# Looking up row numbers for four token tiles per product: diagonal blocks picked by a mask, moved by one small product

## What is computed

```python
capacity = max(1, int(CF * N / E))            # 1.25 * 4096 / 8 = 640
order = jnp.lexsort((-fw, fe))                # by expert, then by falling weight
se, sw, st = fe[order], fw[order], ft[order]  # expert, weight, token
rank = jnp.arange(N * K) - starts[se]
keep = rank < capacity
disp = jnp.zeros((E, capacity + 1, D)).at[se, pos].set(xf[st])
g = jnp.einsum('ecd,edf->ecf', disp, wg)
u = jnp.einsum('ecd,edf->ecf', disp, wu)
eo = jnp.einsum('ecf,efd->ecd', jax.nn.silu(g) * u, wd)
out = jnp.zeros_like(xf).at[st].add(gathered * weight)
```

## Time and profile before

| | |
|---|---|
| median of 3 runs | 659.88 us (659.63 to 659.9) |
| the profiled execution | 656.8 us |
| its span, first to last instruction | 654.9 us |
| TensorE busy | 569.0 us, 87% |
| VectorE busy | 448.4 us, 68% |
| ScalarE busy | 322.0 us, 49% |
| GpSimd busy | 266.4 us, 41% |

### The profile page before, as it was taken

How to read it: one execution, slowest core, us unless ns; L and a number is a source line. 1 busy time by engine, 2 the same in 40 slices (tenths; PEclk the granted TensorE clock), 3 DMA queues, 4 the chain that set the end, 5 groups by cost and what they waited for, 6 DMA issues and landing times.

```text
span 654.9 us, 13692 instructions
## 1 busy us (share of the span) xinstructions
PE 569.0 (87%) x4041; PEld 529.9 (81%) x4041; DVE 448.4 (68%) x1250; ACT 322.0 (49%) x717; POOL 266.4 (41%) x428
## 2 busy tenths in 40 slices
PE   4999889999899401399999999999999999999992
PEld 3677678888777300299999999999999999999992
DVE  3577879898677888875756676677567666666441
ACT  3678768887445510044434445445355354454330
POOL 5588747786678400402025043061070250341321
PEclk9999989999899655589999999999999999999997
DMA  5322258744565640232617336347056174260221
GB/s 169 97 66 73 72 155 269 220 145 132 170 188 189 209 105 0 71 108 82 193 51 159 109 89 137 92 104 185 24 118 195 33 155 129 82 137 9 34 25 16
DMA packets 91911, 75.24 MB, mean 115 GB/s; under 512 B 12108, under 2 KB 88278, under 8 KB 91864
## 3 DMA queue, kind: packets, MB, share of 16 engines
q1 hardware_dynamic: 82872, 58.77, 29.7%
q0 software_dynamic: 8992, 15.90, 12.6%
HBM read 52.48 MB, written 22.16 MB: 114 GB/s over the span
## 4 chain that ended last, share of the span: by engine, by line
PE 63%; DVE 12%; issue 4%; POOL 2%; DMA 2%; ACT 2%; SPq 1%; DVEq 0%; ACTq 0%; POOLq 0%
PE bank L1354 29%; PE bank L1368 14%; PE bank L1389 4%; DVE hit L895 3%; PE bank L1272 3%; PE bank L1175 3%; PE bank L1317 3%; PE bank L1403 2%; PE bank L1331 1%; DVE x L864 1%; PE bank L1252 1%; DVE st L866 1%; DMA w_raw<-wd 1%; PE bank L1261 1%; DMA xg<-h_rows,g_idx 1%
## 5 line engine op out<-in xcount | busy, mean ns | idle before, releaser
L500 POOL DMA_INDIRECT xg<-h_rows,g_idx x40 | 40.8, 1019 | 256.5 <-DVE g_idx L989 246.7
L1354 PE MATMUL bank<-xT_h,w_h 128*128 128x320 f32 x448 | 139.4, 311 | 1.2 <-DVE xT_l L1018 1.2
L1354 PE MATMUL bank<-xT_h,w_l 128*128 128x320 f32 x448 | 138.4, 309 | 0.0
L1354 PE MATMUL bank<-xT_l,w_h 128*128 128x320 f32 x448 | 138.4, 309 | 0.0
L656 ACT CAST hid_h<-hid 128x320 fp32r<-128x320 f32 x112 | 51.7, 461 | 82.5 <-DVE hid L1046 82.5
L1046 DVE TENSOR_TENSOR hid<-act_g,bank 128x320 f32<-128x320 f32 x112 | 54.5, 487 | 54.4 <-ACT act_g L652 54.4
L510 POOL DMA_INDIRECT out<-yo,s_idx x40 | 66.3, 1657 | 60.7 <-DVE yo L1036 21.9
L652 ACT ACTIVATE act_g<-bank 128x320 f32<-128x320 f32 x112 | 48.9, 437 | 82.0 <-PE bank L1354 81.4
L1354 PEld LDWEIGHTS bank<-xT_h,w_h 128*128 128x128 f32 x448 | 84.8, 189 | 1.8 <-issue 1.4
L1354 PEld LDWEIGHTS bank<-xT_l,w_h 128*128 128x128 f32 x448 | 84.6, 189 | 0.0
L1354 PEld LDWEIGHTS bank<-xT_h,w_l 128*128 128x128 f32 x448 | 84.5, 189 | 0.0
(11 more groups left out here) (190 smaller groups left out, 1296.0 us busy)
## 6 DMA issues: line engine op xcount, KB each, us to landing
w_raw<-wg SPq DMA_DIRECT2D x32, 256.0 KB, 3.5
w_raw<-wu SPq DMA_DIRECT2D x32, 256.0 KB, 4.6
w_raw<-wd SPq DMA_DIRECT2D x16, 512.0 KB, 5.7
x_in<-x SPq DMA_DIRECT2D x32, 128.0 KB, 2.1
q_store<-qT SPq DMA_DIRECT2D x32, 128.0 KB, 1.9
q_in<-q_store SPq DMA_DIRECT2D x32, 128.0 KB, 2.1
x_re<-x SPq DMA_DIRECT2D x32, 128.0 KB, 2.1
out<-x SPq DMA_DIRECT2D x32, 128.0 KB, 1.9
```

The costliest lines, as they stand in the source:

```text
L500: nc.gpsimd.indirect_dma_start(out=xg[par][:, a, :], out_offset=None, in_=h2_rows, in_offset=bass.IndirectOffsetOnAxis(ap=g_idx[par][:, a: ...
L1354: last = MM(bank[2 * h + m][:, 0:HCAP], W[i][:, f, at:at + P], XT[j][:, k, cols], start=n == 0, stop=n == 3 * KC - 1)
```

## The change

A slot is now divided by 32 instead of 128: 20 blocks (`BLOCKS`) of 32 rows (`ROWS`). `onehot` has 32 columns per token instead of 128, so the one-hot rows of four token tiles (`Q`) lie side by side as the 128 weight columns of one product, and `facts`, now 2 x 20 = 40 numbers per token tile (`BAND`), of the same four tiles are the 160 streamed columns. A look is 8 products. In the 128 x 160 result only the four diagonal blocks mean something: rows 32q to 32q + 31 with the 40 columns of the q-th tile. `find_diagonal` on VectorE multiplies with the mask `own_q` (`band`) and adds the four blocks (`diag`, 128 x 40). `place` on TensorE, one product with `same_r` (a one wherever two rows are equal modulo 32), sums over the four row groups and gives every group the result. `find_tokens` picks for each row group its column out of four (`spot`, again with `own_q`) and adds the two values.

`own_q`, `fold` and `same_r` are made once on VectorE during attention. ScalarE's copy `iota_b`, a table of 128 x 32 numbers that the old `onehot` was compared with, falls away. `facts_d` counts two parts per expert instead of four.

```diff
-TILE_BITS = 7
+ROWS = 32
+ROW_BITS = 5
+BLOCKS = CAP // ROWS
+Q = P // ROWS
+BAND = NV * BLOCKS
...
+                if s.rep == NT + 5:
+                    with nc.allow_low_precision(reason="zeros and ones"):
+                        RED(own_q[:, :], ident.rearrange("p (q r) -> p q r", q=Q), AX, ALU.add)
+                        link(RED(fold[:, :], ident.rearrange("p (q r) -> p r q", q=Q), AX, ALU.add))
+                    V.tensor_copy(same_r[:, :].rearrange("p (q r) -> p q r", q=Q),
+                                  fold[:, :].unsqueeze(1).to_broadcast([P, Q, ROWS]))
...
-                TT(in_tile[:, :, :], tile_no[:, :].unsqueeze(2).to_broadcast([P, NT, CT]),
-                   tile_id[:, :].unsqueeze(1).to_broadcast([P, NT, CT]), ALU.is_equal).then_inc(in_d, 1)
+                TT(in_block[:, :, :], block_no[:, :].unsqueeze(2).to_broadcast([P, NT, BLOCKS]),
+                   block_id[:, :].unsqueeze(1).to_broadcast([P, NT, BLOCKS]), ALU.is_equal).then_inc(in_d, 1)
...
-                TT(facts[:, sl, :, :], vals[:, sl, :].unsqueeze(3).to_broadcast([P, NT // 2, NV, CT]),
-                   in_tile[:, sl, :].unsqueeze(2).to_broadcast([P, NT // 2, NV, CT]), ALU.mult)
+                TT(facts[:, sl, :, :], vals[:, sl, :].unsqueeze(3).to_broadcast([P, NT // 2, NV, BLOCKS]),
+                   in_block[:, sl, :].unsqueeze(2).to_broadcast([P, NT // 2, NV, BLOCKS]), ALU.mult)
...
-                sl = slice(part * NT // 4, (part + 1) * NT // 4)
-                TT(onehot[:, :, sl], iota_b[:, :, sl], row_in[:, sl].unsqueeze(1).to_broadcast([P, P, NT // 4]),
-                   ALU.is_equal).then_inc(facts_d, 1)
+                sl = slice(part * NT // 2, (part + 1) * NT // 2)
+                TT(onehot[:, sl, :], iota_s[:, 0:ROWS].unsqueeze(1).to_broadcast([P, NT // 2, ROWS]),
+                   row_in[:, sl].unsqueeze(2).to_broadcast([P, NT // 2, ROWS]), ALU.is_equal).then_inc(facts_d, 1)
...
+            def find_diagonal(e):
+
+                dve.wait_ge(look_d, e + 1)
+                TT(band[:, :, :], bank[7][:, 0:Q * BAND].rearrange("p (q n) -> p q n", q=Q),
+                   own_q[:, :].unsqueeze(2).to_broadcast([P, Q, BAND]), ALU.mult).then_inc(band_d, 1)
+                dve.wait_ge(band_d, e + 1)
+                with nc.allow_low_precision(reason="seven bits of each row number are whole and exact"):
+                    RED(diag[:, :], band[:, :, :].rearrange("p q n -> p n q"), AX, ALU.add).then_inc(diag_d, 1)
+
             def find_tokens(e, par):
 
-                dve.wait_ge(look_d, e + 1)
+                dve.wait_ge(place_d, e + 1)
+                TT(spot[:, :].rearrange("p (m q) -> p m q", q=Q),
+                   bank[7][:, Q * BAND:(Q + 1) * BAND].rearrange("p (m q) -> p m q", q=Q),
+                   own_q[:, :].unsqueeze(1).to_broadcast([P, BAND // Q, Q]), ALU.mult).then_inc(spot_d, 1)
+                dve.wait_ge(spot_d, e + 1)
                 with nc.allow_low_precision(reason="row numbers under 4096 are whole and exact"):
-                    RED(g_idx[par][:, :], bank[7][:, 0:NV * CT].rearrange("p (v a) -> p a v", v=NV), AX, ALU.add)\
+                    RED(g_idx[par][:, :], spot[:, :].rearrange("p (v a q) -> p a v q", v=NV, q=Q), AXY, ALU.add)\
                         .then_inc(idx_d, 1)
...
+                    if f == 1 and first:
+                        find_diagonal(1)
+                    if f == FC - 1 and ahead:
+                        find_diagonal(e + 2)
...
-                for n in range(NT):
-                    if n % (NT // 4) == 0:
-                        wait(pe, facts_d, e * 4 + n // (NT // 4) + 1)
-                    last = MM(bank[7][:, 0:NV * CT], onehot[:, :, n], facts[:, n, :, :].rearrange("p v a -> p (v a)"),
-                              start=n == 0, stop=n == NT - 1)
+                for n in range(0, NT, Q):
+                    if n % (NT // 2) == 0:
+                        wait(pe, facts_d, e * 2 + n // (NT // 2) + 1)
+                    last = MM(bank[7][:, 0:Q * BAND], onehot[:, n:n + Q, :].rearrange("p n r -> p (n r)"),
+                              facts[:, n:n + Q, :, :].rearrange("p n v a -> p (n v a)"), start=n == 0, stop=n == NT - Q)
                 last.then_inc(look_d, 1)
+
+            def place(e):
+
+                wait(pe, diag_d, e + 1)
+                MM(bank[7][:, Q * BAND:(Q + 1) * BAND], same_r[:, :], diag[:, :], start=True, stop=True).then_inc(place_d, 1)
...
             look(0)
+            place(0)
...
                     if f == 2 and first:
-                        wait(pe, idx_d, 1)
-                        look(1)
+                        place(1)
...
                 down(e, FC - 1)
+                if ahead:
+                    place(e + 2)
                 gate_up(e + 1, 1 - par, 1)
...
             gate_up(0, 0, 1)
+            pe.wait_ge(idx_d, 1)
+            look(1)
             down(0, 0)
```

More of the change, by code:

```diff
@@ L22 @@
 AX = mybir.AxisListType.X
+AXY = mybir.AxisListType.XY
 B, T, D = 2, 2048, 256
@@ L149, in build_program @@
         same_e = sb("same_e", [P, P], BF16)
+        own_q, same_r = sb("own_q", [P, Q], BF16), sb("same_r", [P, P], BF16)
+        fold = sb("fold", [P, ROWS])
+        band, spot = sb("band", [P, Q, BAND]), sb("spot", [P, BAND])
+        diag = sb("diag", [P, BAND], BF16)
         before, zeros_b = sb("before", [P, P], BF16), sb("zeros_b", [P, P], BF16)
@@ L184, in build_program @@
         vals = sb("vals", [P, NT, NV], BF16)
-        iota_b = sb("iota_b", [P, P, NT], BF16)
-        tile_id = sb("tile_id", [P, CT], I32)
-        in_tile = sb("in_tile", [P, NT, CT])
-        tile_no = sb("tile_no", [P, NT], I32)
+        block_id = sb("block_id", [P, BLOCKS], I32)
+        in_block = sb("in_block", [P, NT, BLOCKS], BF16)
+        block_no = sb("block_no", [P, NT], I32)
         row_in = sb("row_in", [P, NT], BF16)
-        onehot = sb("onehot", [P, P, NT], BF16)
-        facts = sb("facts", [P, NT, NV, CT], BF16)
+        onehot = sb("onehot", [P, NT, ROWS], BF16)
+        facts = sb("facts", [P, NT, NV, BLOCKS], BF16)
         g_idx = [sb(f"g_idx{i}", [P, CT], I32) for i in range(2)]
@@ L297, in build_program @@
         in_d, tn_d, ri_d = sem("in_d"), sem("tn_d"), sem("ri_d")
+        band_d, diag_d, place_d, spot_d = (sem(n) for n in ("band_d", "diag_d", "place_d", "spot_d"))
         facts_d, look_d, idx_d = (sem(n) for n in ("facts_d", "look_d", "idx_d"))
@@ L620, in _ @@
             exp_logits(EARLY, NT)
-            act.wait_ge(plink_s, 8)
-            nc.scalar.copy(iota_b[:, :, :], iota_s[:, :].unsqueeze(2).to_broadcast([P, P, NT])).then_inc(iota_d, 1)
             def split_high(e, f, count, implied=False):
@@ L950, in _, with describe_blocks @@
             place_slots(0)
-            def describe_tiles(e):
+            def describe_blocks(e):
                 sl = slot[:, e, :]
-                V.tensor_scalar(tile_no[:, :], sl, TILE_BITS, None, ALU.arith_shift_right).then_inc(tn_d, 1)
+                V.tensor_scalar(block_no[:, :], sl, ROW_BITS, None, ALU.arith_shift_right).then_inc(tn_d, 1)
                 dve.wait_ge(tn_d, e + 1)
-                TT(in_tile[:, :, :], tile_no[:, :].unsqueeze(2).to_broadcast([P, NT, CT]),
-                   tile_id[:, :].unsqueeze(1).to_broadcast([P, NT, CT]), ALU.is_equal).then_inc(in_d, 1)
-                V.scalar_tensor_tensor(row_in[:, :], tile_no[:, :], -float(P), sl, ALU.mult, ALU.add).then_inc(ri_d, 1)
+                TT(in_block[:, :, :], block_no[:, :].unsqueeze(2).to_broadcast([P, NT, BLOCKS]),
+                   block_id[:, :].unsqueeze(1).to_broadcast([P, NT, BLOCKS]), ALU.is_equal).then_inc(in_d, 1)
+                V.scalar_tensor_tensor(row_in[:, :], block_no[:, :], -float(ROWS), sl, ALU.mult, ALU.add).then_inc(ri_d, 1)
             def describe_facts(e, part):
@@ L1004, in split_low @@
                 V.tensor_tensor(w_l[:, f, :], w_raw[:, f, :], w_h[:, f, :].bitcast(F32), ALU.subtract).then_inc(sp_l, 1)
[L1006 removed]
             describe(0)
+            find_diagonal(0)
             find_tokens(0, 0)
@@ L1056, in describe_ahead @@
                     if f == 2:
-                        describe_tiles(e + 2)
+                        describe_blocks(e + 2)
                     if f in (3, 4):
@@ L1061, in describe_ahead @@
                         describe_rows(e + 2, 0)
+                        describe_rows(e + 2, 1)
                 xf = FC - XG if first else XF
@@ L1066, in expert @@
                     if f == 0 and first:
-                        describe_tiles(1)
+                        describe_blocks(1)
                         describe_facts(1, 0)
-                    if f == 1 and first:
-                        describe_rows(1, 1)
-                        describe_rows(1, 2)
                     if f == 0 and not first:
@@ L1084, in expert @@
                         describe_rows(1, 0)
-                    if f == 1 and first:
-                        describe_rows(1, 3)
```

(7 more changed lines are left out.)

7 lines of the change are left out of this document (2 added, 5 removed).

## The result

The changed kernel takes 651.13 us (median of 9 runs, 649.07 to 655.14), the kernel before beside it 659.67 us (9 runs, 655.35 to 662.85): a ratio of 0.988, 95% interval 0.9861 to 0.9899. The profiled execution took 651.43 us, with a span of 649.3 us.

What follows compares the result with a forecast made beforehand. TensorE, busy 87% of the span and alone on the chain in the middle experts, was taken as the bound. Terms 0.7 + 1.6 + 0.35 - 1.4 - 6.0 = -4.75 us gave 655.1 us from 659.88 us, range 652.0 to 658.2 us.

Steps and rivals of the forecast that it cites:

- the last of the sum: Whole kernel: 652.05 us from the profiled execution, plus the 3.1 us between profile and median, gives 655.1 us.
- Middle experts: Five looks between full experts: each falls from 2.05 to 0.86 us, saving 1.2 us; together -6.0 us.
- Third look: Look behind the wait for expert 1's weights: shorter look, wait unchanged, -1.4 us.
- Routing: First look, serial: nothing covers VectorE's longer work and the four waits in a row, +1.6 us.
- Expert 0: Second look's saving lost to VectorE's queue, with stalls of 0.4 us for `hid`, 0.7 us for `diag`: +0.35 us.
- another rise of the clock there: Start of expert 0: sign of being wrong if the clock, at half until about 282 us, rose at another point.
- Masks: Building `own_q`, `fold`, `same_r` on VectorE in attention, in a chain without slack: +0.7 us (0.3 to 0.8 us).
- The prices: VectorE instructions at the slow rate: `in_block` and `facts` 0.82 us each, `onehot` 0.69 us, `diag` 0.32 us.
- (1): VectorE: fast rate holds for `facts` and `onehot`, helping first look and expert 0; -7.2 us, 652.7 us; 12%.
- (2): TensorE: wide product costs as much as one of 256 columns, `place` 0.4 us; -1.15 us, 658.7 us; 9%.
- (3): TensorE: the new products' weight loads are not hidden, a look takes 3.0 us; +9.9 us, 669.8 us; 4%.
- The lower bound of the product: Look on TensorE: eight products of 160 columns cost at least 8 x 0.062 = 0.5 us.

Runs made afterwards that it cites:

- before: The kernel before, unchanged, in the profile the prediction was made from: profiled execution 656.8 us, span 654.9 us.
- b_again: The kernel before, unchanged, timed and profiled once more: 659.19 us, ratio 1.0009; profile span 656.7 us.
- b_third: The kernel before, unchanged, profiled a third time: one execution, 660.8 us, span 658.9 us.
- after: The changed kernel in its first profile: profiled execution 651.43 us, span 649.3 us; median of runs 651.13 us, ratio 0.988.
- a_again: The changed kernel, unaltered, timed and profiled once more: 650.17 us, ratio 0.987 to the kernel before.
- a_pad: The changed kernel with its new buffers placed behind the old ones, so the others keep their earlier addresses: 649.83 us, ratio 0.9875 to the kernel before.
- a_twice: The changed kernel with every look done twice, 16 products for 8: 656.1 us, ratio 0.9955 to the kernel before.
- b_fourth: The kernel before, unchanged, profiled once more, on the third chip: clock 0.66 behind the third look, `gate_up` there 4.86 us.
- b_wide: The kernel before with 160 streamed columns in each of a look's 32 products, 150 of them unread: 660.71 us, ratio 1.0033.
- b_fifth: The kernel before, unchanged, a further profile: clock 0.70 behind the third look, `gate_up` there 5.16 us.
- b_warm: The kernel before with 12 unread products of 256 columns filling part of the wait ahead of the third look: 658.14 us, ratio 0.999.
- a_spread: The changed kernel with expert 1's list, look and `place` in expert 0 in the old order: 648.78 us, ratio 0.9852 to the kernel before.
- a_early: The changed kernel with the masks built at the program's start instead of late in attention: 650.38 us, ratio 0.9873 to the kernel before.
- a_fast: The changed kernel with the four token tiles innermost in every 2-byte buffer: 648.23 us, ratio 0.9848 to the kernel before.
- a_fill: The changed kernel with 24 unread products of 10 columns ahead of the third look: 652.72 us, ratio 0.9898 to the kernel before.
- a_comb: The changed kernel with token tiles innermost, `in_block` from 2-byte numbers and expert 0's old order, third chip: 654.6 us, ratio 0.9798 to the kernel before.

## Why the prediction was wrong

The stages, in us from the span's start, and what lies between:

| | before | b_again | b_third | after | a_again |
|---|---|---|---|---|---|
| thresholds known (`thr_b`) | 261.3 | 260.5 | 262.9 | 262.2 | 261.6 |
| first `hid` | 283.8 | 282.9 | 285.3 | 286.2 | 285.8 |
| third look | 326.16 | 326.27 | 328.55 | 328.73 | 328.76 |
| last `hid` of the full experts | 597.0 | 598.9 | 601.1 | 591.4 | 591.5 |
| routing | 22.5 | 22.4 | 22.4 | 24.0 | 24.2 |
| expert 0 | 42.4 | 43.4 | 43.3 | 42.5 | 43.0 |
| middle experts | 270.8 | 272.6 | 272.6 | 262.7 | 262.7 |

**The step that failed** is the last of the sum: "the median of the runs is 659.88 us, 3.1 us more, and I take the difference over". The profiled execution of before was not the typical one plus a constant. It lay near the lower end: leaving out the third chip, the kernel before runs from 655.35 to 663.42 us, and its further profiles took 658.68 and 660.8 us. What it lacked did not come back after the change: after, profile and median are 651.43 and 651.13 us. Against its own base the sum gave 652.05 us, within 1 us of both; in part that is luck, since the terms below miss by up to 0.5 us each and in both directions. In place of 3.1 us to carry over, the runs showed that a good part of the difference is a gain:

- The half clock behind the third look costs 4.92 - 3.62 = 1.3 us to 1.5 us, in five of six profiles of kernels with narrow looks there, and the changed kernel doesn't have it. The prediction asks after the clock at the first look and at the start of expert 0 only.
- The period of a middle expert, (552.8 - 371.75) / 4 = 45.26 us by the starts of the looks in my profile, is 45.42 us in the two others: 0.16 us x 5 = 0.8 us. The looks add up to the same; 32 and 33 of the `down` there take 1.77 us, where 21 did in my profile and the rest 1.73 us. The changed kernel shows such a step too (43.97 us, but 43.89 us in `a_pad`). Why it differs stays open.
- Expert 0 takes 42.4 us in my profile and 43.3 us in the others, in part between the request for expert 1's weights and their use (14.8, 15.2 and 15.6 us in the three, 14.4 us after). Over all profiles that wait takes 14.8 to 16.1 us with the narrow look and 14.0 to 15.7 us in the six with the changed order. It scatters from run to run, and that the change has a part in it is not shown. In `b_again` another 0.5 us comes from a clock that rose late (see the terms).

So 1.3 to 1.5 us of the 3.1 us are a gain with a cause, 0.8 us have a place in the traces and no cause, and the rest is not told from scatter.

**The terms.** Middle experts: -6.0 us forecast. The period fell from 45.26 us to (548.65 - 372.77) / 4 = 43.97 us, 1.29 us instead of 1.2 us, so -6.5 us; against 45.42 us it is -7.3 us. The product was right (0.069 us by `a_twice`, the line through the two rows gave 0.068 us, I took 0.075 us); `place` costs 0.13 us for 0.15 us. Mis-sized was what the look takes off the `gate_up` behind it: that is 3.56 us now and not 3.62 us, since the products before it are wide.

Third look: -1.4 us forecast, 2.15 + 3.62 - 0.73 - 3.56 - 0.13 = 1.35 us measured. Routing: +1.6 us forecast, +1.5 to +1.8 us measured. Expert 0: +0.35 us forecast; the stalls were 0.37 us for `hid` and 0.48 us for `diag` (0.4 and 0.7 us forecast), and from the first `hid` to the transposes at f = 5 it is 28.1 us, against 27.6, 28.1 and 27.7 us. The middle one is `b_again`, where the granted clock reached 1.00 only behind the first `hid` (0.50 over the 5 us ahead of it, 0.80 in the first microsecond behind); so it was in `b_fourth` (28.4 us) and `b_wide` (28.5 us), while in `before`, `b_third`, `b_fifth` and `b_warm` (27.6 to 27.7 us), and in all ten kernels with the new look, it stood at 1.00 by then. Like with like the stretch is 0.5 us longer after the change, near the forecast 0.35 us, and `a_spread` (27.1 us) shows that the order is what eats the gain. The prediction had named another rise of the clock there as a sign of being wrong; it moves some executions of before, not the changed kernel.

Masks: +0.7 us forecast (0.3 to 0.8 us), 0.4 us in the traces. By the starts of `st`, thirteen tiles at the end of attention take 35.3 to 35.4 us in all nine profiles that build the masks there, and 34.9 to 35.0 us in `a_early` and in all but one of the profiles with the old look (35.1 us in `b_fifth`). The three instructions keep VectorE for 0.8 us; half of that falls into time in which its `x` would have waited for TensorE (0.26 to 0.39 us at the tiles beside), which the forecast took as not there. `a_early` was not faster for it: its last tile waited for a transfer, so that it stands 3.25 us behind the tile before, where it is 2.4 to 3.4 us in the profiles of the other kernels with the new look, without a pattern.

**The prices.** `in_block`, `facts` and `onehot` came at 825, 818 and 684 ns, as forecast at the slow rate; `a_fast` confirms the reason by removing it. With that the rule of the Trainium skill ("Vector Engine (DVE) Microarchitecture Reference", section 5.1), an innermost step of one for the packed mode, agrees with the runs on both sides. `diag` was 439 ns and not 320 ns: I had priced a reduction by its number of elements, and this one reads them in steps of 40; where `a_fast` reads them side by side it takes 320 ns.

**The rivals.** (1), the fast rate, was not what the change does, but its worth was right: -7.2 us against -4.75 us is 2.45 us, and `a_fast` gains some 2.4 us in routing and expert 0. (2), dear products or a dear `place`, is refuted by `a_twice` and the chain. (3), exposed weight loads, is refuted by the changed look itself, 0.57 us for eight, and by `b_wide`, where 32 loads each hide behind a product at 0.072 us. (Its terms add up to +9.7 us, 6.0 + 1.0 + 2.65, and not to +9.9 us.) The lower bound of the product, "more columns cannot be cheaper", rested on 0.062 us for a narrow one; with `a_fill` at 0.032 us it was no bound, though nothing came out below it. The side of the result was right.

Added up against usual executions of before: +0.4 us for the masks, +1.7 us for routing, nothing that can be told for expert 0, -272.6 + 262.7 = -9.9 us for the middle experts (the half clock and the third look with them), 7.8 us in all; measured 8.5 us.

## What to carry to other kernels

A difference between the profiled execution and the median is not a constant of the program: part of it can be a stall or a clock that this one execution happened to miss, and a change that removes its cause keeps it as a gain. Profile the kernel before two or three times, or look at each place where TensorE waits and then streams little, before a sum is set against it. Where a broadcast operand has 2 bytes, put the axis that doesn't repeat innermost: here that was worth some 2.4 us by the stages, and the list's place in expert 0 1.1 us, beside 8.5 us for the change itself; the two remove the same stalls in expert 0 and don't add there. Where many narrow products follow each other, look also at how their weight columns lie: a load took 168 ns here with columns 64 bytes apart and 96 to 102 ns with columns side by side.

## What was not expected of the hardware

- 2 us of products with 10 columns behind a wait of 1.3 to 2.2 us were followed, in five of six profiles, by a clock of 0.66 to 0.70 over 5 us; the same number of products with 160 columns behind a wait of 1.97 us by 1.00, and 2 us of products with 10 columns without a wait ahead by 1.00 too.
- A product of 160 columns follows the next after 0.069 to 0.072 us, one of 10 columns after 0.062 us, each with its own load of 128 x 128 weights whose columns lie 64 bytes apart: 150 more columns cost 0.01 us. With the weight columns side by side, and the same weights each time, one of 10 columns follows after 0.032 us.
- On the third chip the same kernel took 668.36 us instead of 658.4 us. Its profile has VectorE standing still once or twice per middle expert (nine times for 1.0 to 4.6 us in `b_fourth`, three times in `a_comb`, never for over 1 us in `before`, `b_again` and `after`) with nothing in the profile to release it, and the period of an expert is 47.1 us there instead of 45.4 us. One of them, in `b_fourth`:

```profile
396.51 0.49 DVE L1046 TENSOR_TENSOR hid<-act_g,bank 128x320 f32<-128x320 f32 x1 [3.12 <-issue]
```

What VectorE does in these 3.12 us stays open, and so does whether it belongs to the chip or to the hour.
